# Row scatter of a four-layer graph network: 62 groups shared out anew over six stages

## What is computed

```
x = _layernorm(x + L0(x))   # three attention layers in a row, 4 heads
x = _layernorm(x + L1(x))   # node sum: segment_sum(x[src], dst) + (1+eps) x, two-layer MLP, column norm
x = _layernorm(x + L2(x))   # dot attention over the edges, 4 heads
msg = relu(x[src] + edge_attr @ We + be)           # L3, edge messages
h = x + segment_sum(msg, dst)                       # then two-layer MLP, column norm, x = _layernorm(x + ...)
```

## Time and profile before

| | us |
|---|---|
| median of 3 runs | 6648.32 |
| lowest to highest | 6645.05 to 6662.31 |
| the profiled execution | 6664.46 |
| its span, first to last instruction | 6662.7 |

### The profile page before, as it was taken

How to read it: one execution, slowest core, us unless ns; L and a number is a source line. 1 busy time by engine, 2 the same in 40 slices (tenths; PEclk the granted TensorE clock), 3 DMA queues, 4 the chain that set the end, 5 groups by cost and what they waited for, 6 DMA issues and landing times. The chain is left out here.

```text
span 6662.7 us, 64336 instructions
## 1 busy us (share of the span) xinstructions
PE 3526.5 (53%) x23063; PEld 2140.3 (32%) x23064; DVE 3951.5 (59%) x4332; ACT 2501.6 (38%) x3930; POOL 3974.1 (60%) x3115
## 2 busy tenths in 40 slices
PE   3112221110537888578885778876788633434344
PEld 2111111110524444344443444444333222323222
DVE  3435543332789897598975999755899811212123
ACT  1000000000437778477774777731666401111111
POOL 2888888887517666276662766620880066666662
PEclk6555555555668899788987889888788756666666
DMA  7222222222978887388963889762322111121211
GB/s 262 19 19 19 19 11 8 0 0 10 343 240 195 206 206 152 100 197 204 213 146 90 196 205 210 162 183 93 104 83 70 40 43 45 44 46 44 45 43 22
DMA packets 402266, 722.19 MB, mean 108 GB/s; under 512 B 171741, under 2 KB 249483, under 8 KB 397854
## 3 DMA queue, kind: packets, MB, share of 16 engines
q0 software_dynamic: 231840, 286.03, 28.0%
q1 hardware_dynamic: 166894, 430.81, 18.9%
q10 hardware_dynamic: 3216, 1.23, 0.1%
HBM read 603.52 MB, written 114.31 MB: 108 GB/s over the span
## 5 line engine op out<-in xcount | busy, mean ns | idle before, releaser
L331 POOL DMA_INDIRECT counts<-plcell_add,plcell_slot x806 | 1258.4, 1561 | 393.2 <-issue 225.0
L1630 POOL DMA_INDIRECT emxg<-xtab,emsrc x832 | 809.0, 972 | 442.7 <-issue 246.0
L1698 DVE TENSOR_TENSOR emmsg<-emps_m,emxg 128x384 f32<-128x384 f32 x208 | 115.9, 557 | 1023.7 <-remote 773.0
L1747 PE MATMUL emps_a<-emmsg,emsame 128*128 128x96 f32 x1664 | 302.1, 340 | 760.4 <-issue 367.5
L706 ACT ACT_TABLE_LOAD x1 | 1.3, 1283 | 1616.8 <-PE mtps L694 1616.8
L423 DVE TENSOR_REDUCE plnlow<-plsame 128x13 f32<-128x1664 bf16 x62 | 117.0, 1888 | 818.1 <-DMA counts<-plcell_add,plcell_slot 818.0
L1747 PEld LDWEIGHTS emps_a<-emmsg,emsame 128*128 128x128 f32 x1664 | 278.8, 249 | 895.3 <-issue 889.3
L1140 PE MATMUL ga0psE<-ident,ga0logit 128*128 128x128 f32 x2500 | 401.1, 299 | 205.3 <-DMA ga0logit<-log_counts 124.0
L347 PE MATMUL plrows<-ident,plcell 128*128 128x128 f32 x806 | 174.2, 401 | 633.0 <-DVE plsame L417 632.3
L1140 PE MATMUL ga1psE<-ident,ga1logit 128*128 128x128 f32 x2500 | 402.1, 300 | 194.7 <-DMA ga1logit<-log_counts 121.8
L1140 PE MATMUL ga2psE<-ident,ga2logit 128*128 128x128 f32 x2500 | 399.6, 299 | 196.8 <-DMA ga2logit<-log_counts 127.1
(11 more groups left out here) (349 smaller groups left out, 8824.7 us busy)
## 6 DMA issues: line engine op xcount, KB each, us to landing
ga0logit<-log_counts POOLq DMA_DIRECT2D x88, 512.0 KB
ga1logit<-log_counts POOLq DMA_DIRECT2D x88, 512.0 KB
ga2logit<-log_counts POOLq DMA_DIRECT2D x88, 512.0 KB
counts<-plzeros SPq DMA_DIRECT2D x32, 1250.0 KB
mthalf<-counts SPq DMA_DIRECT2D x50, 800.0 KB
log_counts<-mtlogs SPq DMA_DIRECT2D x25, 1600.0 KB
ga0near<-log_counts SPq DMA_DIRECT2D x50, 800.0 KB
ga1near<-log_counts SPq DMA_DIRECT2D x50, 800.0 KB
```

Source lines behind the costliest of these rows:

```text
L331: nc.gpsimd.indirect_dma_start(counts[w][:, :], bass.IndirectOffsetOnAxis(ap=cell_slot[:, g % 2, j:j + 1], axis=0), cell_add[:, g % 2, j:j ...
L1630: nc.gpsimd.indirect_dma_start(xg[:, h, t, :], None, xtab[:, :], bass.IndirectOffsetOnAxis(ap=src[:, h, t:t + 1], axis=0)).then_inc(gather ...
L1698: nc.vector.tensor_tensor(msg[:, v % RING, :, :].rearrange("p t d -> p (t d)"), ps_m[:, v % 2, 0:CT * D], xg[:, g % XG, lo:lo + CT, :].rea ...
L1747: last = nc.tensor.matmul(flat_a[:, bass.ds(lo, D)], same[:, v % RING, t, :], msg[:, v % RING, t, :], start=False, stop=(v == CHUNKS - 1 a ...
```

## The change

The 62 groups are divided anew, and the node sum gets a share:

| stage | groups before | groups after | scatters before | after |
|---|---|---|---|---|
| tables | 3 | 6 | 39 | 78 |
| each attention layer | 16 | 10 | 208 | 130 |
| node sum | 0 | 6 | 0 | 78 |
| dot stage | 11 | 20 | 143 | 260 |

```
-TABLE_GROUPS = (0, 3)
-LAYER_GROUPS = ((3, 19), (19, 35), (35, 51))
-DOT_GROUPS = (51, 62)
+TABLE_GROUPS = (0, 6)
+LAYER_GROUPS = ((6, 16), (16, 26), (26, 36))
+GIN_GROUPS = (36, 42)
+DOT_GROUPS = (42, 62)
...
-def gin_pool(nc, a, x, xT, halves_rows):
+def gin_pool(nc, a, x, xT, halves_rows, edges):
...
+        scatter, _ = edge_scatter(nc, ctx, a, edges, "gins", *GIN_GROUPS)
         with nc.Block() as block:
+            @block.gpsimd
+            def _(pool):
+                for _ in scatter(pool):
+                    pass
+
```

More of the change, by code:

```diff
@@ L158, in program @@
         transpose_and_project(nc, "t1", x, ident, xT)
-        gin_pool(nc, a, x, xT, halves_rows)
+        gin_pool(nc, a, x, xT, halves_rows, edges)
         mlp_norm(nc, a, "L1_gnn", ident, xT, y)
```

## The result

The kernel after takes **6724.09 us** (median of 4 runs, 6720.78 to 6726.13) against 6655.32 (4 runs of before on the same chip, 6645.05 to 6667.98): ratio **1.0102, 95% interval 1.0081 to 1.0123**. A second timing of the same two gave 6717.62 (6 runs) against 6660.22: 1.0092, 1.0074 to 1.0109. So it is some 57 to 69 us slower where the prediction said 36, and 60 at most: the direction is right, the size is not.

What follows compares the result with a forecast made beforehand. DMA bounds the tables, VectorE the attention layers and dot stage, TensorE the node sum; GpSimd ends no stage. Terms 41 + 1 + 2 - 15 + 6 = +35 us gave 6684 us against 6648.3; range 6656 to 6708.

Steps and rivals of the forecast that it cites:

- Node sum, scatter's pace: Node sum: held-up scatters end 0.84 us after VectorE's addition, two per 5.38 us period; last issued by about 4607.
- the rival in which scatters hold VectorE up: Attention layers and dot stage: scatters ahead of VectorE delay it about 0.5 us each; sum -33 us, 6615; chance 0.02.
- the one in which scatters fit better: Node sum: held-up scatters end 0.05 us behind VectorE, three per period; node sum costs 17 us, total 6659; chance 0.06.
- Node sum, the end: Node sum's block end: 2.5 us for the last scatter's landing (1 to 5.6), within the stage's +41 us (37 to 46).
- The MLP: MLP behind the node sum: first product pass slower after TensorE idles about 40 us; +1 us, bounds 0 and 3.
- Tables: Tables: 39 more scatters barely covered, more load on busy DMA engines; +2 us, bounds 0 and 8.
- Attention layers: Three attention layers: fewer group changes (3.5 us) and mask waits (1.5 us) per layer; -15 us, bounds -4 and -59.
- the attention layers give back more: Attention layers: mask waits come mostly from GpSimd or scatter traffic; from 17 us per layer, no slower; chance 0.12.
- Dot stage: Dot stage: 117 more scatters, covered with 35 us to spare, slow VectorE's products; +6 us, bounds 3 and 9.
- More than one stage spills: Tables' last group ends behind the store, node sum's loads held up: 8 and 10 us more, 6700 to 6712; chance 0.10.
- sign of being wrong: Wrong if an attention layer shortens by over 12 us, or the node sum's GpSimd is through before 4590.
- signs of being right: Included about 40 us from node sum's last VectorE operation to next load, and each attention layer 3 to 8 us shorter.

Runs made afterwards that it cites:

- late3: Shares 3/15/3/11 against before's 3/16/0/11 (tables/each layer/node sum/dot stage), node sum's scatter begun only after 21 of 25 additions; node sum and MLP 235.2 us.
- noatt: Kernel before with the scatter's 48 groups in the three attention layers left out altogether; 6637.38 us, ratio 0.9967.
- gin5: Against before, five groups in the node sum; 3 in tables, 14, 15, 14 in the layers, 11 in dot stage; node sum and MLP 224.1 us.
- gin4: Against before, four groups in the node sum; 3 in tables, 15, 15, 14 in the layers, 11 in dot stage; node sum and MLP 205.1 us.
- light: As gin6only, but VectorE's node-sum addition reads one of the two count tables only; node sum and MLP 206.7 us.
- gin6only: Kernel before with six groups in the node sum, 14 in each attention layer, tables and dot stage unchanged; 6705.64 us, ratio 1.0059.

## Why the prediction was off

Step by step, against the table of stages.

- **Node sum, scatter's pace: right.** The last scatter was to be issued by about 4607 before the shift of the stages ahead. It started at 4598.20, with the additions starting at 4420.9 where they started at 4427.4, a shift of 6.5: it would be 4604.7, its end 4605.7. The rule (0.84 us behind VectorE's end, two scatters per long period, 17 to 19 us per group once VectorE is through) held to 2 us over 180, and not by luck: counted from the stage's start, the six groups ended at 52, 91, 129, 152, 170 and 187 us for a forecast of 55, 93, 131, 151, 170 and 188. VectorE's additions were hardly slowed (median 3.493 us before and after): 19 of the 25 began inside a scatter, 17 of these took 3.49 us and two 3.63. So the rival in which scatters hold VectorE up for half a microsecond each has no support in this stage, and the one in which scatters fit better is refuted by rows such as 4519.10.
- **Node sum, the end: mis-sized, and it is the step that failed first.** "GpSimd waits for its landing ... so I take 2.5 us, at least 1 and at most 5.6", with 0.7 us to the next load, gave 3.2 us from the last scatter's start to that load. It was 10.7, which is 7.5 us too little. The forecast had the landing in this term, but not the 7.57 us that GpSimd's DRAIN takes behind it. The bound came from the end of the first stage, the only end of a GpSimd block that before shows uncovered; it was no bound, since in this stage the end grows from 6.0 us at 39 scatters to 9.7 at 78, and the DRAIN of the first stage took 2.55 us. Before's own trace has a DRAIN of 3.90 us behind 39 scatters, under cover in the tables. A further 1.5 us come at the other end: the first addition starts 9.1 us after the stage's first operation in after, 8.9 to 9.6 in the kernels whose scatter begins with the stage, and 7.4 to 7.8 in those without one and in late3, whose GpSimd is idle then. GpSimd's six loads and the first blocks' loads lie side by side there; that they are the cause is read from the kernels' grouping, not tried by itself. From VectorE's last addition to the next load it is 17.7 us in before and 63.4 in after, 45.7 more; with 1.5 at the start and 0.8 in the MLP that is the stage's 48.
- **The MLP: right.** Its first pass took 8.93 us where it took 8.13: +0.8 for a forecast of +1. The granted clock over the node sum, its tail included, was 0.86 where it was 0.95, of the full 2.4 GHz.
- **Tables: +4.6 for +2, inside its bounds of 0 and 8, but by a wrong reason.** "Its data is little beside the stage's 336 GB/s" weighed bytes in a stage whose engines are full. The time of packets is the measure. In the DMA view the software queue, which carries the scatter and its loads, took this share of the 16 engines' time in the tables before and after (packets, MB, share):

```profile
q0 software_dynamic: 1600, 1.38, 2.2%
...
q0 software_dynamic: 3152, 2.76, 4.3%
```

  2.1% more of 250 us is 5.2 us, and the hardware queue's part fell from 95.3% to 93.3%. In a stage that DMA bounds, this comes straight on top.
- **Attention layers: -6 for -15, 9 us and the largest miss of all.** The gain was the mis-sized term, in both of its parts. Six group changes at 0.58 us were to give 3.5 us of VectorE's time per layer; its busy time fell by 2.2 to 2.5. And 1.5 us per layer were to come back through TensorE's waits for masks, "near the lower end"; noatt shows that even with no scatter these waits stay. So the true lower end, nothing, was the answer, and the rival "the attention layers give back more" falls with it: the entire scatter of 48 groups is worth 16.4 us here, so 18 groups could not have brought 51. The individual layers moved by +4.4, -7.0 and -3.4 us; the totals of kernels with nearly equal shares lie between 2476.7 (gin5) and 2493.0 (gin4), so -6 is known to about its own size and agrees with 18 x 0.34 = 6.
- **Dot stage: +7.4 for +6, right.** Beside the scatter VectorE did 102 and 101 products in two windows of 250 us, as many as the earlier trace rows shows with it and 2 to 3 fewer than without (the last scatter started at 5297.4, 40 us before the stage's last work, for a forecast of 30):

```profile
4740.00:4990.00 250.00, 151.70 (x102) 0.82 0.26 81
5000.00:5250.00 250.00, 151.16 (x101) 0.84 0.26 82
```

- **The sum.** With the measured terms, 48.2 + 4.6 - 6.0 + 7.4 = 54 us, against 42 + 2 - 15 + 6 = 35 forecast. Measured against the medians it is 57 and 69. The 19 us between 54 and 35 are 6 in the node sum, almost all of them its end, 9 in the attention layers, 3 in the tables and 1 in the dot stage. The rest, 3 to 15 us, lies in the spread of executions and in the open question on the edge messages; no run settles it. "More than one stage spills" is the rival that came nearest in time (6700 to 6712), but not by its mechanism: the tables' scatters were through at 1882, 25 us before the stage's end, and of the 10 us that it gave the node sum's loads at most the 1.5 us at the start are there. Neither sign of being wrong came (no layer was 12 us shorter, and GpSimd was through at 4599): both asked for errors other than the two that were made. Of the signs of being right, "about 40 us" from VectorE's last operation to the next load was 46.4, and one layer got longer by 4.4 us where each was to get shorter by 3 to 8.

One sum in the rivals is off: "VectorE is held up" at -33 leaves out the MLP, the tables and the +6 of the dot stage that its own 58 replaces; by its own terms it is 41 + 1 + 2 - 15 - 117 + 58 = -30. Nothing hangs on it.

The range, up to 60 us over before, failed narrowly: one timing has 69 us and the other 57. Three terms leaned the same way (the end of the node sum, the layers, the tables), its upper end stood on one measured bound that didn't bound (5.6 us), and a spread of before's own runs of 17 us, from 6645 to 6662, was not in it.

## What to carry over

Before a stage is given asynchronous work as a filler, lay the work into its gaps operation by operation, and add what the engine needs at the block's end, taken from a block that has issued the same kind and number of DMAs; as long as both end under cover the filler is nearly free (three groups, 1 to 2 us), and beyond that each microsecond is paid in full (six groups, 48 us). Ask first what the work costs where it is: leaving out all 48 groups from the attention layers gained 16 us, so moving 18 of them could gain 6, whatever the busy times say. In a stage bound by DMA count a transfer by the time its packets take, not by its bytes against the rate.

## What the runs showed of the hardware

- The end of a block in which GpSimd has issued indirect DMAs takes GpSimd time after all of them have landed: 6.03, 7.29, 8.48 and 9.74 us from the last one's end to the next engine's first load for 39, 52, 65 and 78 of them, 0.095 us each. A DRAIN of GpSimd makes up 3.90, 5.12, 6.34 and 7.57 us of it. Outside this span of counts it goes otherwise: 5.61 us for 143, 8.22 for 260.
- An indirect DMA of GpSimd is held up by VectorE's 1.83 us operation on one tensor (16-bit integers to f32) just as by the 3.49 us addition of two, and ends 0.81 to 0.84 us behind it. VectorE's operations get hardly longer (1.827 and 3.493 us median). Single ones do, by up to 0.24 us in light and 0.32 in gin6only, eight and four of the 25 there, and none in the kernels without a scatter in this stage; in light five of the eight began inside a scatter. The Trainium skill ("SBUF — State Buffer", "SBUF: two separate sides") has whichever engine comes first block the other; for GpSimd's waits these runs agree. For VectorE's they don't as a rule: 17 of the 19 additions of after that began inside a scatter took their 3.49 us. Whether the few longer ones are such waits was not tried.
- 78 scatters in place of 39, with their loads, took 2.1% more of the 16 DMA engines' time for 1.38 MB more, in a stage that moves 84 MB, and the stage got 4.6 us longer.
